# A chain of four attention layers on one core: reordered outputs, split work and fc1 order at two seams

## The reference, cut to what matters

```python
def _forward(x, xf_1, xf_2, ...):            # both contexts are the same tensor
    h = _layer_norm(x, ln1_scale, ln1_offset)
    x = x + _cross_attention(h, xf_1, wq1, ..., bias_k1, bias_v1)   # 16 heads of 128
    h = _layer_norm(x, ln2_scale, ln2_offset)
    x = x + _cross_attention(h, xf_2, wq2, ..., bias_k2, bias_v2)
    h = _layer_norm(x, ln_mlp_scale, ln_mlp_offset)
    h = jax.nn.gelu(h @ w_fc1 + b_fc1, approximate=False) @ w_fc2 + b_fc2   # 256 -> 1024 -> 256
    return x + h
```

## Time and profile before

| | us |
|---|---|
| median of 3 runs | 979.11 |
| the three runs | 977.96, 979.20, 979.11 |
| the profiled execution | 978.71 |
| its span, first to last instruction | 976.9 |
| TensorE busy (96%) | 939.9 |
| VectorE busy (60%) | 590.4 |
| ScalarE busy (47%) | 463.3 |
| GpSimd busy (43%) | 416.9 |
| mean granted clock | 0.995 |

### The profile page before, as it was taken

The page is one execution under the profiler, slowest core; times in us unless marked ns, Lnnn a source line. Parts: engine busy times, 40 slices in busy tenths (PEclk is TensorE's granted clock), DMA queues, the critical chain, the costliest instruction groups (busy, mean ns, idle before and its releaser), DMA issues.

```text
span 976.9 us, 21455 instructions
## 1 busy us (share of the span) xinstructions
PE 939.9 (96%) x8300; PEld 791.9 (81%) x8300; DVE 590.4 (60%) x974; ACT 463.3 (47%) x1026; POOL 416.9 (43%) x572
## 2 busy tenths in 40 slices
PE   6999999988999999999999999999999999999998
PEld 4777777976789888998897888898888888678776
DVE  5899986768434443344465443344436766999883
ACT  4677875258543334233343333333332434566565
POOL 2164345858366243342257343342322862343231
PEclk9999999999999999999999999999999999999999
DMA  9100000320021111111101111111100100000000
GB/s 294 43 23 2 2 2 15 124 55 2 1 59 52 48 54 28 48 38 48 55 7 55 50 54 40 35 38 48 54 23 17 50 6 1 1 2 6 13 6 22
DMA packets 24146, 37.13 MB, mean 38 GB/s; under 512 B 4432, under 2 KB 16528, under 8 KB 23824
## 3 DMA queue, kind: packets, MB, share of 16 engines
q1 hardware_dynamic: 24080, 36.23, 12.2%
HBM read 35.17 MB, written 1.05 MB: 37 GB/s over the span
## 4 chain that ended last, share of the span: by engine, by line
PE 76%; DVE 11%; ACT 4%; issue 4%; POOL 4%; DMA 0%; SPq 0%; DVEq 0%; ACTq 0%; POOLq 0%
PE ps L1295 18%; PE ps L790 14%; PE ps L1312 9%; PE ps L1354 6%; PE ps L1965 5%; PE ps L892 4%; PE ps L1330 4%; PE ps L1340 2%; DVE sb L2493 2%; DVE sb L656 1%; PE ps L270 1%; PE ps L421 1%; PE ps L2043 1%; DVE sb L650 1%; PE ps L372 1%
## 5 line engine op out<-in xcount | busy, mean ns | idle before, releaser
L837 POOL TENSOR_TENSOR sb<-sb 128x256 fp32r<-128x256 f32 (+1 forms) x128 | 102.5, 801 | 279.2 <-DMA sb<-in_heads_a 142.6
L1295 PE MATMUL ps<-sb 128*128 128x512 f32 x768 | 187.9, 396 | 1.0 <-issue 1.0
L1295 PEld LDWEIGHTS ps<-sb 128*128 128x128 f32 x768 | 139.5, 188 | 33.1 <-ACT sb L1428 3.1
L790 PE MATMUL ps<-sb 128*128 128x256 f32 x1152 | 148.6, 286 | 0.0
L790 PEld LDWEIGHTS ps<-sb 128*128 128x128 f32 x1152 | 141.3, 191 | 2.0 <-issue 0.2
L839 POOL TENSOR_TENSOR sb<-sb 128x256 fp32r<-128x256 f32 (+1 forms) x128 | 115.3, 901 | 10.0
L1525 DVE SCALAR_TENSOR_TENSOR sb<-ps,sb 128x512 fp32r<-128x512 f32 x64 | 45.1, 746 | 96.3 <-ACT sb L1461 96.2
L1312 PE MATMUL ps<-sb 128*128 128x256 f32 x768 | 99.2, 285 | 0.4 <-DVE sb L1493 0.4
L1505 DVE TENSOR_REDUCE sb<-ps 128x8 f32<-128x520 f32 x32 | 22.4, 699 | 126.6 <-PE ps L1330 126.6
L1312 PEld LDWEIGHTS ps<-sb 128*128 128x128 f32 x768 | 95.0, 191 | 3.0 <-issue 0.9
L1428 ACT ACTIVATE sb<-ps,sb 128x512 f32<-128x512 f32 x64 | 43.8, 685 | 107.8 <-PE ps L1295 107.7
(11 more groups left out here) (221 smaller groups left out, 1663.8 us busy)
## 6 DMA issues: line engine op xcount, KB each, us to landing
sb<-in_heads_a SPq DMA_DIRECT2D x32, 386.0 KB, 3.0
sb<-in_heads_c SPq DMA_DIRECT2D x16, 256.0 KB, 3.6
sb<-in_heads_b SPq DMA_DIRECT2D x32, 128.0 KB, 3.0
sb<-in_mlp_a SPq DMA_DIRECT2D x16, 128.5 KB, 2.1
sb<-in_mlp_b SPq DMA_DIRECT2D x16, 128.0 KB, 2.2
sb<-in_w_r SPq DMA_DIRECT2D x1, 2048.0 KB, 7.7
sb<-in_encT SPq DMA_DIRECT2D x1, 1024.0 KB, 6.7
sb<-in_ctx SPq DMA_DIRECT2D x1, 1024.0 KB, 8.1
```

What stands on the lines that cost most here:

```text
L790: last = pe.matmul(m.acc(t), lhsT[x], rhs[w], start=opens and n == 0, stop=False, skip_group_check=True)
L837: pool.tensor_tensor(high, src, one, ALU.mult).then_inc(*G.did(name + "_high", u))
L1295: last = pe.matmul(m.ps[u][:, c, :], m.w_parts[u][w][:, (KD * q + k) * P:(KD * q + k + 1) * P], rows[x][:, k, c * 512:(c + 1) * 512], star ...
```

## The change

In the last round of an attention TensorE takes the tiles in another order: stream 0 tiles 0, 2, 1, 3, 4, 6, stream 1 tiles 0, 2, 1, 3, then `s_half`, then stream 0's tiles 5, 7 and stream 1's 4, 6, 5, 7. Each stream waits for both of its low parts ahead of its first tile. In the first seam, for half 1, ScalarE writes the high part of the two tiles that VectorE scales, behind VectorE's scaling, in place of VectorE's copy. In the second seam, for half 0, VectorE makes the low part that GpSimd made, between its `rows(0)` and `normed(1)`. TensorE runs nine filler products between the turns and then round 0's fc1 of half 0 for both streams, ahead of the second turn; the MLP's own list starts one step later.

```diff
@@ seam_vector, rows
-        for k in range(KD):
+        by_scalar = new and c == 1
+        for k, name in zip(range(KD), ("hT", "high")):
             last = vec.tensor_scalar(m.hT[:, k, cols].rearrange("p (t q) -> p t q", q=P), m.turned(1, c, k), m.col(scale, k), m.col(shift, k), ALU.mult,
                                      ALU.add)
-        last.then_inc(*V.did("hT", c))
-        vec.wait_ge(*V.at("hT", c, 0))
-        vec.tensor_copy(m.h_parts[0][:, :, cols], m.hT[:, :, cols]).then_inc(*V.did("high", c))
+            if by_scalar:
+                last.then_inc(*V.did(name, c))
+        if by_scalar:
+            vec.wait_ge(*m.own_act.at("seam_high", seam))
+        else:
+            last.then_inc(*V.did("hT", c))
+            vec.wait_ge(*V.at("hT", c, 0))
+            vec.tensor_copy(m.h_parts[0][:, :, cols], m.hT[:, :, cols]).then_inc(*V.did("high", c))
...
+    def low(c):
+        first = slice(4 * c * P, (4 * c + 2) * P)
+        vec.wait_ge(*A.at("high", c, 0))
+        vec.tensor_tensor(m.h_parts[1][:, :, first], m.hT[:, :, first], m.h_parts[0][:, :, first].bitcast(F32),
+                          ALU.subtract).then_inc(m.s_h[c], 1)
...
         rows(0)
+        low(0)
         normed(1)
         rows(1)
@@ seam_gpsimd
-    for c in range(2):
+    for c in halves:
         low(c)
@@ seam_tensor
     if not new:
-        warm(10)
+        warm(9)
+        for u in range(STREAMS):
+            fc1(pe, mlp, m, 12, u, 0, 0)
@@ seam_scalar
+    def others_high(c):
+        cols = slice((4 * c + 2) * P, (4 * c + 4) * P)
+        act.wait_ge(*ph.vec.at("high", c, 0))
+        for k in range(KD):
+            last = act.activation(m.h_parts[0][:, k, cols].rearrange("p (t q) -> p t q", q=P), m.turned(1, c, k),
+                                  ACT.Identity, bias=m.col(shift, k), scale=m.col(scale, k))
+        last.then_inc(*m.own_act.did("seam_high", 1))
...
     rows(1)
+    if new:
+        others_high(1)
@@ heads_tensor
+    def last_outs(r):
+        for u in range(STREAMS):
+            pe.wait_ge(*hd.out.pool.at("wb", u, r))
+            for o in range(2):
+                pe.wait_ge(*V.at(f"ctx_low{o}", u, r))
+            last = out_tiles(u, (0, 2, 1, 3) if u else (0, 2, 1, 3, 4, 6), False)
+        last.then_inc(m.s_half, 1)
+        out_tiles(0, (5, 7), False).then_inc(*hd.out.pe.did("out", 0))
+        out_tiles(1, (4, 6, 5, 7), False).then_inc(*hd.out.pe.did("out", 1))
...
-            for u in range(STREAMS):
-                for half in range(2):
-                    out(u, r, first, half)
+            last_outs(r)
@@ gpsimd
-            seam_gpsimd(pool, ph["norm2"], m, 1)
+            seam_gpsimd(pool, ph["norm2"], m, 1, (0, 1))
...
-            seam_gpsimd(pool, ph["norm3"], m, 2)
+            seam_gpsimd(pool, ph["norm3"], m, 2, (1,))
@@ tensor
-            seam_tensor(pe, ph["norm3"], heads[2], None, m)
-            mlp_tensor(pe, ph["mlp2"], m, 12, HALVES[:-LATE])
+            seam_tensor(pe, ph["norm3"], heads[2], None, m, ph["mlp2"])
+            mlp_tensor(pe, ph["mlp2"], m, 12, HALVES[1:-LATE])
```

More of the change, by code:

```diff
@@ L1044, in seam_vector, with seam_gpsimd @@
         rows(0)
+        low(0)
         normed(1)
         rows(1)
-def seam_gpsimd(pool, ph, m, seam):
+def seam_gpsimd(pool, ph, m, seam, halves):
     own = m.own_pool
@@ L1072, in seam_gpsimd, with seam_tensor @@
         rstd(c)
-    for c in range(2):
+    for c in halves:
         low(c)
-def seam_tensor(pe, ph, old, new, m):
+def seam_tensor(pe, ph, old, new, m, mlp=None):
     V, A = ph.vec, ph.act
@@ L1357, in context, with out_tiles, out @@
         last.then_inc(*hd.main.pe.did("ctx", u))
-    def out(u, r, first, half=None):
-        if half != 1:
+    def out_tiles(u, these, first):
+        for t in these:
+            last = into_acc(pe, m, t, [x[u][:, t, :] for x in m.cT_parts], [x[:, :] for x in m.wb_parts[u]],
+                            first and u == 0)
+        return last
+    def out(u, r, first):
+        pe.wait_ge(*hd.out.pool.at("wb", u, r))
+        for o in range(2):
+            pe.wait_ge(*V.at(f"ctx_low{o}", u, r))
+            last = out_tiles(u, range(o, TILES, 2), first)
+        last.then_inc(*hd.out.pe.did("out", u))
+    def last_outs(r):
+        for u in range(STREAMS):
             pe.wait_ge(*hd.out.pool.at("wb", u, r))
-        for o in range(2):
-            if half != 1:
+            for o in range(2):
                 pe.wait_ge(*V.at(f"ctx_low{o}", u, r))
[L1367 to L1373, removed]
+            last = out_tiles(u, (0, 2, 1, 3) if u else (0, 2, 1, 3, 4, 6), False)
+        last.then_inc(m.s_half, 1)
+        out_tiles(0, (5, 7), False).then_inc(*hd.out.pe.did("out", 0))
+        out_tiles(1, (4, 6, 5, 7), False).then_inc(*hd.out.pe.did("out", 1))
     def enter():
```

## The result

| | before | after |
|---|---|---|
| median, us (20 runs each) | 979.12 | 981.33 |
| profiled execution, us | 978.71 | 982.28 |
| its span, us | 976.9 | 980.3 |

The ratio is 1.0021, 95% interval 1.0012 to 1.0029: about 2.1 us slower. The spans of single executions differ by some us outside the seams too (the outputs ahead of the first seam begin at 493.72 before and at 494.66 after, where nothing was changed). So I compare marks inside the seams, counted from the first output product of the attention ahead. Two marks carry the document: in the first seam the first scores product; in the second the end of the last fc1 product that the earlier trace rows shows, 786.56 + 3.18 before.

The account below looks back on a forecast made before the run. TensorE, with 76% of the chain, was taken as the bound, GpSimd level with it behind the second seam. First seam -1.0 and second +1.8 gave +0.8 us, 978.7 to 979.5; range 979.0 to 980.4.

Parts of the forecast that it names:

- the clock's: Second seam, second half's fc1: cost of a fall to 1.2 GHz, between nothing and 1.71 us, taken as 1.1.
- the wait behind the turn: Second seam: TensorE idles 3.6 us before the second half's fc1, twice the 1.78 behind which the clock fell.
- rival B: Second seam: the clock stays low for two stretches of 3.4 us; total +3.0, 981.7 us; chance 0.08.
- The first seam: From one attention's last head to the next's second query product: 1.0 us gained, lower bound 0.6.
- VectorE's scalings start at 511.93 - 0.6: First seam: the first half's sums, 0.6 us sooner, bring VectorE's scalings forward by as much, to 511.33.
- the wait ahead of the second query product: First seam: TensorE's 1.00 us wait would be gone or below 0.2.
- ScalarE's part: First seam: two ScalarE activations, about 1.0 us, replace VectorE's copy, which took 1.42.
- The two levels: Second seam: the later of TensorE, 1.7 us late, and GpSimd, 1.4 late, sets the last fc1; 1.8 lost.
- rival A: Second seam: GpSimd catches up its 1.4 us of lateness; total -0.4, 978.3 us; chance 0.20.
- the last fc1 would still wait for GpSimd's weights: Second seam, sign after the change: the last fc1's wait for GpSimd's split weights, 0.27 us before, remains.
- The turn: Second seam: the second turn, behind fc1 of the first half, comes at 760.1 in place of 758.70, 1.4 us later.
- the bubble in the outputs: Second seam: the new output order leaves TensorE waiting 0.1 to 0.2 us for stream 1's odd low part.

Follow-up runs that it names:

- E7: The kernel before with only the new order of the outputs, in both seams; time ratio to the kernel before 0.9995.
- E2: The changed kernel with 14 filler products added behind the second turn; last fc1 ends at 48.57 us after the outputs began, against 50.14 in the changed kernel.
- E9: The changed kernel with 14 fillers behind the second turn and GpSimd's bias adds of the first half behind the last weights; ratio to the kernel before 1.0013.
- E5: The kernel before with 18 fillers in place of 10 between the second seam's turns; last fc1 ends at 47.12 us after the outputs began, against 47.14.
- E6: The changed kernel with 7 filler products added behind the second turn; last fc1 ends at 48.53 us after the outputs began.
- E1: The changed kernel with the first half's fc1 behind the second turn again and ten fillers ahead of it; 978.77 us against 978.67 for the kernel before.

## Why the prediction was wrong

**The term that was mis-sized** is the clock's, in "What that costs lies between nothing ... and 7.34 - 5.63 = 1.71 ... I take 1.1". That the wait behind the turn would be 3.6 and the clock fall there was right (3.40). But I took the kernel before's single low stretch for the most that could follow. Its cost was 2.58 + 0.22 = 2.8 in one execution and 1.70, the upper end of my bounds, in the other. TensorE, 0.5 late at the start of the second half's fc1 (0.6 forecast), ended 3.0 or 1.9 late in place of 1.7, with the wait of 0.27 ahead of the last fc1 gone. The first of the two is the mechanism of rival B, at 0.08, with 981.7 as its time; the median was 981.33. The wait was nearly twice the one in the earlier trace rows, and that was a reason to take both stretches into the range.

**The first seam** was forecast at 1.0 and gave 0.76. The step that failed is "VectorE's scalings start at 511.93 - 0.6": I carried the earlier sums through the whole chain without reading GpSimd's list ahead of the scales. E7 shows 0.11 for them, and the wait ahead of the second query product, forecast as gone or below 0.2, was 0.32. ScalarE's part worked as costed: 1.02 for its two activations (1.0 forecast), 0.69 for the subtraction. The fall in the sum, 0.24, is small, but the reason behind it was wrong.

**The two levels** held in part. GpSimd's lateness was forecast at 1.4, and E2, with the clock full, ends 1.43 late. That agreement is partly luck: GpSimd was free 22.02 - 20.08 = 1.94 late in E2, its subtraction longer than forecast, and had caught up 0.5 by the last fc1 weights, as rival A had it on a larger scale. E9 takes only 0.4 back by relieving GpSimd, since VectorE, which the forecast counted in no level, is as late. The forecast's sign that the last fc1 would still wait for GpSimd's weights did not come in the changed kernel, where TensorE was later. E5 confirms that the low stretch of the kernel before cost nothing.

**The turn** was 1.46 late (1.4 forecast), fc1 in front of it began at 757.74, 0.37 later than worked out, with outputs that began 0.38 later, so as forecast; the bubble in the outputs was 6.21 - 6.02 = 0.19 (0.1 to 0.2); the sums in the second seam came 0.53 sooner (0.6). VectorE came first at the shared subtraction, by 0.08, the case that was left open. The GPSIMD Engine Reference of the Trainium skill (Key points) says that GpSimd contends with VectorE instructions that have two SBUF inputs. The 1.74 against 1.27 agrees with it, a second case beside the earlier trace rows and in the other direction.

With the measured terms, -0.76 + 1.9 to 3.0 is +1.2 to +2.2; the medians show +2.2 and +2.0. The upper end fits, so the longer stretch may be the commoner one; two profiled executions don't settle it, and falls of the clock elsewhere are in the medians too.

## What to carry to other kernels

Work moved ahead of a step to fill a wait also delays that step when its own operands come late: ask when it can start, not only whether TensorE is idle there. A wait that is filled in one place and opened, longer, in another can also cost the clock; seven fillers were worth 0.5 to 1.6 us at the mark here, and not moving the work 2.4 to 3.5. Where one late step feeds several engines, relieving one of them uncovers the next. And an earlier input is worth nothing until the list of each engine on the way has been read: GpSimd's queue took nearly all of it in one seam and none in the other.

## What the runs showed of the hardware

Behind the same 3.40 us of waiting the low clock lasted 6.8 us in one execution and 3.4 in another, and began 1.0 us ahead of the products in one and 0.4 behind their start in the other. With the wait cut to 1.79 by fillers (E6) there was none, while 1.78 of idle time in the kernel before had brought one and 2.06 in E1 brought none, each in one execution: the length of one wait alone does not tell whether the clock falls. At the low parts of the second half, the engine that began its subtraction second, by about 0.1 us, lost 0.5 us (GpSimd, 1.74 in place of 1.27) or 1.0 us (VectorE, 1.71 in place of 0.69).
